# The short convolution of a Mamba block moves from VectorE to TensorE, as four shifted products with scaled weights

## Chip, core and metric

The kernel runs on one core of a Trainium2 chip. The metric is device time in microseconds (us); lower is better. The kernel before took 253.39 us in the median of 3 runs (253.25 to 253.78).

## What is computed

There are 4 sequences of 256 tokens with 256 features (`x`), and a context with 128 features per token (`ctx`). The first half is a Mamba block on the context:

```
x   = einsum('ed,bld->bel', in_proj_w, ctx)           # 128 -> 256 channels
xc  = causal convolution of x along the tokens, 4 taps per channel (depthwise)
u   = silu(xc + conv_b)
dt, B, C = x_proj_w @ u                               # 8 + 16 + 16 rows
delta = softplus(dt_proj_w @ dt + dt_proj_b)
state = state * exp(delta*A) + delta*u*B              # scan over 256 tokens, 16 states per channel
y   = (sum over states of state*C + D*u) * silu(layernorm(x))
x   = x + tanh(g_xattn) * y
```

The second half is a feed-forward part on layernorm(x): 2 shared units and 8 experts of width 176, of which the two best experts of each token count. Its result is added to x with tanh(g_ffn).

The convolution is xc[e, l] = sum over k = 0..3 of conv_w[e, k] * x[e, l - 3 + k]. Since x is itself a product with `in_proj_w`, the same value is the sum over k of (conv_w[e, k] * in_proj_w[e, :]) times ctx of token l - 3 + k.

## The kernel before

The Mamba part is cut into five pieces of tokens: pieces 0 and 1 are the halves (128 tokens) of the first sequence, pieces 2, 3 and 4 the other three sequences (256 tokens each). The 256 channels lie in two halves of 128 partitions. The scan is cut into 64 steps of 128x512 elements, 16 for each sequence; each step is two states for both channel halves and 128 tokens. The feed-forward part works on 8 tiles of 128 tokens with 10 units each ("up" on TensorE, "gate" on ScalarE and VectorE, "mul" on VectorE, "turn" and "down" on TensorE).

Every engine executes its tasks in a fixed order that is written out in the table `ORDER` as `task:number`. An engine never passes a waiting task. Semaphores join the engines.

The tasks that matter here:

- `project:p` (TensorE, L570): 2 products of `win` with `ctx`, one for each channel half, into PSUM. For piece 1 the result begins three tokens early, since the taps look back.
- `project_out:p` (ScalarE, L723): copies from PSUM, scaled by half of the last tap, plus half the bias, into `xh`. It has two instructions.
- `tap0`, `tap1`, `tap2` (VectorE, L907): each adds one shifted tap from PSUM into `xh`, in two instructions. With five pieces there are 30 instructions.
- `tanh_u` (ScalarE, L729) and `silu_u` (VectorE, L917): u = (tanh(xh) + 1) * xh, which is silu since xh holds half the value.
- `xproj`, `dt`, `dt_out`, `soft_exp`, `log_1`, `soft_log`, `log_2`, `delta0`, `delta1`, `delta2`: they give delta and du = delta*u. `xproj` also writes B and C to DRAM, from where they come back broadcast to all partitions (`bb`, `cc`).
- `scan:m`: on ScalarE it stands for the four exponentials of step m + 1 (L704), on GpSimd for the product dbu = du*B of step m + 1 (L1061), and on VectorE for the scan instruction of step m (L953).
- `prod:m`: VectorE's product with C (L963). Its sum is made on TensorE for the first 8 steps (L600) and on GpSimd afterwards (L1104).
- `keep_ends`, `carry`, `fix`: they carry the state from the first half of a sequence into the second.
- `z_stats:i`: mean and variance of `x` of sequence i, on VectorE (L971, L974) and then GpSimd (L1127 to L1133). `z_norm` and `z_gate` use them.
- `variance:t` (VectorE L1010, GpSimd L1149 to L1155), `norm:t` (ScalarE L807) and `to_features:t` (TensorE L635): they bring tile t to the feed-forward part.

At the start SyncE's queue loads `ctx` of the first sequence, small weights, `x` of the first sequence, the other `ctx`, and then the other three `x`. ScalarE's queue loads `win` and then `params`. TensorE runs 6 products of zeros before `project:0`, 11 after `project:1`, and one before `dt:0`.

## Time and profile before

| | value |
|---|---|
| median of 3 runs | 253.39 us |
| profiled execution | 253.55 us, its span 251.7 us |
| TensorE busy | 205.5 us (82%) |
| VectorE busy | 215.0 us (85%) |
| ScalarE busy | 171.2 us (68%) |
| GpSimd busy | 195.3 us (78%) |
| mean granted clock of TensorE | 0.919 |

The profile shows one execution. Busy time is summed over the whole span, though different stretches are limited by different engines, so the shares must be read by stretch. A granted clock of 1.00 is 2.4 GHz, and 0.50 is 1.2 GHz.

### The profile page before, as it was taken

The page shows a single profiled execution, that of the slowest core. Times are in us where ns is not written, and L with a number is a line of the kernel's source. Part 1 is how long each engine was busy: PE and PEld are TensorE (multiplying, and loading weights), DVE is VectorE, ACT ScalarE, POOL GpSimd, SP SyncE. Part 2 cuts the span into 40 slices and gives each one's busy share as a digit, 9 for nine tenths or more (in the row PEclk, how much of TensorE's full clock was granted, in tenths as well). Part 3 has the DMA queues.
Part 4 walks back from the last instruction along what each step waited for, and adds up shares of the span by engine and source line. Part 5 has one row for each costly group of instructions (what it writes and reads, how often), then busy time and mean ns, then how long its engine had stood idle before and what let it go on. Part 6 is the DMA issues. An engine that isn't in the chain of part 4 may idle for free. (4 is left out here: it accounts for less than half of the span.)

```text
span 251.7 us, 3757 instructions
## 1 busy us (share of the span) xinstructions
PE 205.5 (82%) x874; PEld 148.7 (59%) x874; DVE 215.0 (85%) x522; ACT 171.2 (68%) x508; POOL 195.3 (78%) x237
## 2 busy tenths in 40 slices
PE   8534594658669895677996899889999999999995
PEld 4223273434355662345854587568888778788884
DVE  2789999999998989999999999989999999645340
ACT  4579879997758997458757998676775682343220
POOL 0248889999999999999999999999999996510000
PEclk9855579575979999999999999999999999999999
DMA  6496999770490202002209302020300000000000
...
DMA packets 26821, 25.45 MB, mean 101 GB/s; under 512 B 1064, under 2 KB 25904, under 8 KB 26160
## 3 DMA queue, kind: packets, MB, share of 16 engines
...
q10 hardware_dynamic: 288, 0.16, 0.2%
...
HBM read 24.04 MB, written 1.18 MB: 100 GB/s over the span
## 5 line engine op out<-in xcount | busy, mean ns | idle before, releaser
L1061 POOL TENSOR_TENSOR dbu<-du,bb 128x512 f32<-128x512 f32 x64 | 81.3, 1284 | 5.1 <-DVE du L463 3.3
L704 ACT ACTIVATE psA<-delta,aneg 128x127 f32<-128x127 f32 x256 | 78.0, 358 | 5.6 <-DVE psH L953 5.3
L953 DVE TENSOR_TENSOR_SCAN psH<-psA,dbu 128x512 f32<-128x512 f32 x64 | 76.5, 1218 | 1.5 <-POOL dbu L1087 0.4
L667 PE MATMUL psU<-wup,hnT 128*128 128x352 f32 x176 | 63.6, 491 | 12.8 <-DVE hcat L869 8.9
L1104 POOL TENSOR_TENSOR acc<-acc,prod 128x512 f32<-128x512 f32 x42 | 54.5, 1297 | 2.4 <-DVE prod L963 1.8
L545 PE MATMUL psD<-wdn,hT 128*128 128x256 f32 x224 | 52.2, 380 | 0.6 <-issue 0.6
L667 PEld LDWEIGHTS psU<-wup,hnT 128*128 128x128 f32 x176 | 32.8, 200 | 32.8 <-DVE hcat L869 13.6
L833 ACT ACTIVATE tg<-psU 128x176 f32<-128x176 f32 x80 | 24.4, 314 | 36.7 <-PE psU L667 23.9
L545 PEld LDWEIGHTS psD<-wdn,hT 128*128 128x128 f32 x224 | 41.5, 190 | 6.7 <-issue 1.1
L963 DVE TENSOR_TENSOR prod<-psH,cc 128x512 f32<-128x512 f32 x64 | 41.9, 679 | 1.1 <-POOL acc L1104 0.7
L1035 DVE SCALAR_TENSOR_TENSOR ag<-tg,psU 128x176 f32<-128x176 f32 x80 | 25.5, 330 | 15.5 <-ACT tg L833 15.1
L869 DVE SCALAR_TENSOR_TENSOR hcat<-psU,wtok,ag 128x176 f32<-128x176 f32 x64 | 24.2, 395 | 0.9
L840 ACT COPY hT<-psM 128x512 f32<-128x512 f32 (+1 forms) x32 | 16.1, 502 | 11.5 <-PE psM L645 11.0
L678 PE MATMUL psU<-whi,hnhi 128*128 128x352 f32 x56 | 23.3, 415 | 0.2 <-DVE hcat L869 0.2
L645 PE MATMUL psM<-ident,hcat 128*128 128x128 f32 x112 | 18.2, 280 | 2.3 <-ACT hT L840 1.4
L645 PEld LDWEIGHTS psM<-ident,hcat 128*128 128x128 f32 x112 | 13.8, 142 | 7.5 <-issue 2.0
L680 PE MATMUL psU<-whi,hnlo 128*128 128x352 f32 x56 | 18.1, 323 | 0.0
L679 PE MATMUL psU<-wlo,hnhi 128*128 128x352 f32 x56 | 18.0, 322 | 0.0
L600 PE MATMUL psD<-prod,ident 128*128 128x256 f32 x32 | 11.2, 516 | 3.3 <-DVE prod L963 3.3
L663 PE MATMUL psU<-wup,hnT 128*128 128x360 f32 x32 | 12.4, 514 | 0.6 <-ACT hnT L815 0.5
L678 PEld LDWEIGHTS psU<-whi,hnhi 128*128 128x128 f32 x56 | 10.6, 188 | 2.8 <-DVE hcat L869 1.0
L600 PEld LDWEIGHTS psD<-prod,ident 128*128 128x128 f32 x32 | 8.1, 265 | 6.7 <-issue 4.8
(117 smaller groups left out, 282.9 us busy)
## 6 DMA issues: line engine op xcount, KB each, us to landing
...
```

Of the source, the lines that this page charges most:

```text
L545: last = pe.matmul(psD[:, 0:D], hT[0:m, g % HT_RING, c:c + P], wdn[0:m, f, :], start=(f == 0), stop=(f == FB - 1))
L645: last = pe.transpose(psM[0:m, c:c + P], hcat[:, t % 2, f * P:f * P + m], ident[:, :])
L667: last = pe.matmul(dst, hnT[:, b % 2, k, lh * P:(lh + 1) * P], wup[:, j - 1, k, :], start=(k == 0), stop=(k == KT - 1))
L678: pe.matmul(dst, h_hi, w_hi, start=(k == 0), stop=False)
L704: last = act.activation(dst[:, j, h, 1:], delta[:, b % 2, h, l0 + 1:l1], ACT.Exp, scale=aneg[:, h * DS + s0 + j:h * DS + s0 + j + 1])
L833: act.activation(tg[:, i % 2, :], psU[:, i % 2, 0:FF], ACT.Tanh, scale=0.5).then_inc(s_tanh, 1)
L869: last = dve.scalar_tensor_tensor(dst, up, wtok[:, b % 2, lh, j - 2:j - 1], ag[:, unit % 2, :], ALU.mult, ALU.mult)
L953: dve.tensor_tensor_scan(psH[:, i % 2], psA[:, i % DA_RING], dbu[:, i % DBU_RING], 0.0, ALU.mult, ALU.add).then_inc(s_scan, 1)
L963: dve.tensor_tensor(tile(prod[:, i % PROD_RING], i), tile(psH[:, i % 2], i), c.unsqueeze(2).broadcast_to([P, ns, EH, l1 - l0]), ALU.mult). ...
L1035: dve.scalar_tensor_tensor(ag[:, i % 2, :], tg[:, i % 2, :], 1.0, psU[:, i % 2, 0:FF], ALU.add, ALU.mult).then_inc(s_ag, 1)
L1061: pool.tensor_tensor(tile(dbu[:, m % DBU_RING], m), du[:, b % 2, :, l0:l1].unsqueeze(1).broadcast_to(shape), bb[:, b % 2, s0:s0 + ns, l0:l ...
L1104: pool.tensor_tensor(acc[:, total % 2], before, prod[:, i % PROD_RING], ALU.add).then_inc(s_add, 1)
```

## The change

The taps leave VectorE. At the start, `in_proj_w` is multiplied by each of the four taps, two products on VectorE (taps 3 and 1) and two on GpSimd (taps 2 and 0). For this the tap weights are loaded, broadcast to all partitions, into a buffer that the scan uses later. Each projection then issues 8 products instead of 2, four for each channel half. The four add up in PSUM, each with the context shifted by its tap. `project_out` scales by 0.5 and adds the bias, and `tanh_u` waits for it directly. The order table is written anew for all engines except SyncE.

```diff
 "TensorE":
-        project:0 project:1 xproj:0 dt:0 xproj:1 dt:1 project:2 prod:0 prod:1 xproj:2 prod:2 prod:3 prod:4
-        prod:5 dt:2 prod:6 prod:7 y_sum:0 to_tokens:0 to_features:0 project:3 up:0 up:1 up:2 up:3 up:4 xproj:3
+        project:0 project:1 xproj:0 dt:0 xproj:1 dt:1 project:2 prod:0 xproj:2 prod:1 prod:2 prod:3 prod:4 dt:2
+        prod:5 prod:6 prod:7 y_sum:0 to_tokens:0 project:3 to_features:0 up:0 up:1 up:2 up:3 xproj:3 up:4 turn:0
 "ScalarE":
-        load:0 project_out:0 project_out:1 tanh_u:0 xproj_out:0 tanh_u:1 dt_out:0 soft_exp:0 xproj_out:1
-        soft_log:0 dt_out:1 soft_exp:1 soft_log:1 first:0 scan:0 skip:0 project_out:2 scan:1 scan:2 z_norm:0
+        load:0 project_out:0 z_norm:0 project_out:1 tanh_u:0 tanh_u:1 skip:0 xproj_out:0 dt_out:0 soft_exp:0
+        xproj_out:1 soft_log:0 dt_out:1 soft_exp:1 soft_log:1 first:0 scan:0 scan:1 scan:2 z_gate:0
...
+        scan:14 weights_hi:3 norm:0 to_features_out:0 project_out:3 z_norm:1 logits_out:0 gate:0 gate:1 tanh_u:3
+        scan:15 z_gate:1 scan:16 weights_hi:4 scan:17 gate:2 gate:3 decay:1 scan:18 xproj_out:3 gate:4 gate:5
 "VectorE":
-        load:0 tap0:0 tap1:0 tap2:0 silu_u:0 tap0:1 tap1:1 tap2:1 z_stats:0 silu_u:1 z_stats:1 log_1:0 z_stats:2
-        z_stats:3 log_2:0 delta0:0 delta1:0 log_1:1 delta2:0 log_2:1 delta0:1 scan:0 scan:1 delta1:1 keep_ends:0
+        load:0 z_stats:0 z_stats:1 z_stats:2 z_stats:3 silu_u:0 silu_u:1 log_1:0 log_2:0 delta0:0 delta1:0
+        delta2:0 log_1:1 log_2:1 delta0:1 scan:0 scan:1 keep_ends:0 prod:0 prod:1 keep_ends:1 scan:2 delta1:1
+        scan:3 delta2:1 prod:2 prod:3 keep_ends:2 keep_ends:3 silu_u:2 scan:4 scan:5 prod:4 keep_ends:4
+        keep_ends:5 scan:6 prod:5 prod:6 scan:7 keep_ends:6 prod:7 keep_ends:7 scan:8 scan:9 prod:8 z_gate:0
 "GpSimd":
-        z_stats:0 z_stats:1 first:0 scan:0 scan:1 z_stats:2 z_stats:3 scan:2 scan:3 scan:4 scan:5 scan:6 scan:7
+        load:0 z_stats:0 z_stats:1 z_stats:2 z_stats:3 first:0 scan:0 scan:1 scan:2 scan:3 scan:4 scan:5 scan:6
...
-        scan:47 scan:48 prod:45 variance:4 prod:46 fold:5 features_lo:4 prod:47 fold2:5 gate_y:5 scan:49 scan:50
+        scan:47 variance:4 scan:48 prod:45 prod:46 fold:5 features_lo:4 prod:47 fold2:5 gate_y:5 scan:49 prod:49

+        taps = prod[:, 0:2, :].rearrange("p r (k d) -> p (r k) d", d=DI)
+        def scale_tap(engine, k):
+            if k >= 2:
+                engine.wait_ge(d_win, 16)
+                engine.wait_ge(d_taps, 16)
+            engine.tensor_tensor(wk[:, k], win[:, :], taps[:, k], ALU.mult).then_inc(s_wk[k % 2], 1)
 # project, TensorE
-                    dst, lo = entry(i)
                     for h in range(EH):
-                        last = pe.matmul(dst[:, h, :], win[:, h * P:(h + 1) * P], ctx_sb[:, b, lo:l1],
-                                         start=True, stop=True)
+                        for k in reversed(range(DC)):
+                            back = DC - 1 - k
+                            if i == 0 and h == 0:
+                                pe.wait_ge(s_wk[k % 2], 2 - k // 2)
+                            n0 = max(l0, back)
+                            last = pe.matmul(entry(i)[:, h, n0 - l0:], wk[:, k, h * P:(h + 1) * P],
+                                             ctx_sb[:, b, n0 - back:l1 - back], start=(k == DC - 1), stop=(k == 0))
 # ScalarE, ahead of all else
+            act.dma_start(taps[:, :, :], w_taps.unsqueeze(0).broadcast_to([P, DC, DI])).then_inc(d_taps, 16)
             act.dma_start(win[:, :], w_in).then_inc(d_win, 16)
 # project_out
-                        act.activation(xh[:, h, l0:l1], src[:, h, l0 - lo:], ACT.Identity,
-                                       scale=Wh[:, h, DC - 1:DC],
-                                       bias=cwh[:, EH * DC + h:EH * DC + h + 1]).then_inc(s_xh, 1)
+                        act.activation(xh[:, h, l0:l1], entry(i)[:, h, :], ACT.Identity,
+                                       scale=0.5, bias=cwh[:, h:h + 1]).then_inc(s_xh, 1)
 # VectorE: load gets scale_tap(dve, k) for k in (3, 1), GpSimd's new load:0 scale_tap(pool, k) for k in (2, 0)
-                elif task in ("tap0", "tap1", "tap2"):
...
-                        dve.scalar_tensor_tensor(xh[:, h, n0:l1], src[:, h, n0 - back - lo:l1 - back - lo],
-                                                 Wh[:, h, k:k + 1], xh[:, h, n0:l1],
-                                                 ALU.mult, ALU.add).then_inc(s_tap, 1)
```

## Rows read from the trace of the kernel before

**Rows 1.** The page's first part: busy us, share of the span, instructions.
```profile
PE 205.5 (82%) x874; PEld 148.7 (59%) x874; DVE 215.0 (85%) x522; ACT 171.2 (68%) x508; POOL 195.3 (78%) x237
```
**Rows 2.** Windows: stretch and length, busy time by engine, granted clock, DMA share, GB/s.
```profile
52.85:161.00 108.15, 85.70 (x340) 57.89 (x340) 103.34 (x239) 83.93 (x253) 106.20 (x117) 0.95 0.27 88
161.00:222.30 61.30, 59.69 (x297) 48.00 (x298) 56.08 (x148) 37.38 (x119) 52.69 (x68) 1.00 0.09 27
```
**Rows 3.** Timeline of the two hand-overs: start, length, engine, line, what.
```profile
160.99 0.21 POOL L1149 TENSOR_SCALAR ve<-mv 128x1 f32<-128x1 f32 x1
...
220.41 0.60 ACT L807 ACTIVATE hn<-x_sb,nb,rs 128x256 f32<-128x256 f32 x1 [0.27 <-POOL nb L1155]
...
222.30 0.38 PE L635 MATMUL psD<-ident,hn 128*128 128x128 f32 x2
```
**Rows 4.** Timeline of the start, from the projection to GpSimd's products.
```profile
4.45 0.61 PE L570 MATMUL psD<-ctx_sb,win 128*128 128x131 f32 x4
4.65 0.81 ACT L723 ACTIVATE xh<-psM,cwh 128x128 f32<-128x128 f32 x2 [0.36 <-PE psM L570]
...
7.57 0.42 DVE L917 SCALAR_TENSOR_TENSOR u<-psM,xh 128x256 f32<-128x256 f32 x1 [0.45 <-ACT psM L729]
...
9.99 1.28 ACT L731 ACT_TABLE_LOAD   x1
...
10.71 0.74 DVE L971 BATCH_NORM_STATS2 zst<-x_sb 128x6 f32<-128x256 f32 x2
...
15.18 0.39 DVE L932 SCALAR_TENSOR_TENSOR dnc<-dy,psH 128x256 f32<-128x256 f32 x1
...
17.23 3.90 POOL L1061 TENSOR_TENSOR dbu<-du,bb 128x512 f32<-128x512 f32 x3 [3.33 <-DVE du L463]
...
18.71 2.54 DVE L953 TENSOR_TENSOR_SCAN psH<-psA,dbu 128x512 f32<-128x512 f32 x2
...
24.65 4.94 POOL L1061 TENSOR_TENSOR dbu<-du,bb 128x512 f32<-128x512 f32 x4
```
**Rows 5.** Instructions on `xh`: count, ns min/median/max, first and last start.
```profile
L907 DVE SCALAR_TENSOR_TENSOR xh<-psM,cwh,xh x24: 339/470/480, 5.5 to 98.5; 128x253 f32<-128x253 f32 x6, 128x254 f32<-128x254 f32 x6, 128x255 f32<-128x255 f32 x6, 128x125 f32<-128x125 f32 x2
L907 DVE SCALAR_TENSOR_TENSOR xh<-psD,cwh,xh x6: 343/343/343, 7.9 to 9.2; 128x128 f32<-128x128 f32 x6
```
**Rows 6.** GpSimd's waits in 17 to 163 us: total, times, longest.
```profile
POOL dbu L1061 <- DVE psH L953: 1.8, 4, 1.0
```
**Rows 7.** A window (0.50 is the granted clock) and two projections of 256 columns.
```profile
17.20:24.65 7.45, 3.50 (x8) 2.36 (x9) 7.19 (x14) 7.43 (x24) 6.76 (x11) 0.50 0.69 194
...
17.81 2.07 PE L570 MATMUL psM<-ctx_sb,win 128*128 128x256 f32 x4 [3.37 <-DVE dnc L932]
...
89.00 1.03 PE L570 MATMUL psM<-ctx_sb,win 128*128 128x256 f32 x4
```
**Rows 8.** Issue of `x`; us to landing of lines 500 and 477; window 6:7.
```profile
3.42 1.46 SPq L477 DMA_DIRECT2D x_sb<-in_x  x3
...
DMA to landing us min/median/max: 3.5/4.9/10.0
DMA to landing us min/median/max: 4.1/4.3/4.4
6.00:7.00 1.00, 1.00 (x6) 0.47 (x5) 1.00 (x5) 0.16 (x1) 0.00 (x0) 1.00 1.03 343
```
**Rows 9.** Two-input products from SBUF: alone, beside GpSimd, and GpSimd's own.
```profile
15.60 0.42 DVE L452 TENSOR_TENSOR dnc<-drel,dnc 128x256 f32<-128x256 f32 x1
...
17.79 0.99 DVE L452 TENSOR_TENSOR dnc<-drel,dnc 128x256 f32<-128x256 f32 x1
...
118.09 0.73 POOL L1137 TENSOR_TENSOR hnlo<-hnT,hnhi 128x256 fp32r<-128x256 f32 x1
```
**Rows 10.** Timeline of VectorE at `scan:8` and `prod:8`.
```profile
38.07 2.33 DVE L953 TENSOR_TENSOR_SCAN psH<-psA,dbu 128x512 f32<-128x512 f32 x2
...
40.63 1.27 DVE L963 TENSOR_TENSOR prod<-psH,cc 128x512 f32<-128x512 f32 x2
```

More of the change, by code:

```diff
@@ L162 @@
-        z_gate:0 scan:3 tanh_u:2 decay:0 scan:4 scan:5 xproj_out:2 weights_hi:0 scan:6 z_norm:1 scan:7 scan:8
-        dt_out:2 weights_hi:1 soft_exp:2 scan:9 scan:10 soft_log:2 norm:0 scan:11 to_features_out:0 scan:12
-        project_out:3 scan:13 logits_out:0 gate:0 gate:1 z_gate:1 weights_hi:2 weights_hi:3 scan:14 skip:1
-        gate:2 weights_hi:4 scan:15 tanh_u:3 decay:1 scan:16 scan:17 gate:3 gate:4 scan:18 xproj_out:3 hidden:0
-        gate:5 scan:19 scan:20 gate:6 gate:7 hidden:1 scan:21 scan:22 dt_out:3 skip:2 gate:8 gate:9 soft_exp:3
@@ L167 @@
-        scan:23 soft_log:3 norm:1 scan:24 hidden:2 hidden:3 scan:25 scan:26 z_norm:2 to_features_out:1
-        project_out:4 z_gate:2 logits_out:1 gate:10 gate:11 scan:27 scan:28 skip:3 decay:2 tanh_u:4 gate:12
-        scan:29 gate:13 gate:14 scan:30 gate:15 gate:16 scan:31 gate:17 scan:32 hidden:4 hidden:5 scan:33
-        gate:18 gate:19 norm:2 to_features_out:2 features_hi:2 scan:34 scan:35 hidden:6 logits_out:2 gate:20
-        gate:21 scan:36 skip:4 hidden:7 scan:37 scan:38 gate:22 gate:23 xproj_out:4 scan:39 scan:40 gate:24
@@ new lines @@
+        logits_out:1 gate:10 project_out:4 tanh_u:4 skip:3 gate:11 gate:12 gate:13 scan:28 scan:29 gate:14
+        gate:15 scan:30 scan:31 gate:16 hidden:4 hidden:5 decay:2 gate:17 scan:32 gate:18 z_norm:2 gate:19
+        scan:33 scan:34 norm:2 to_features_out:2 features_hi:2 z_gate:2 skip:4 scan:35 logits_out:2 gate:20
+        gate:21 scan:36 hidden:6 hidden:7 gate:22 scan:37 scan:38 gate:23 gate:24 scan:39 xproj_out:4 gate:25
+        scan:40 norm:3 hidden:8 to_features_out:3 gate:26 gate:27 hidden:9 scan:41 scan:42 skip:5 features_hi:3
@@ L195 @@
-        keep_ends:21 mul:7 prod:21 gate_y:1 scan:22 scan:23 gate:8 residual:1 gate:9 stats:1 variance:1
-        keep_ends:22 log_1:3 keep_ends:23 prod:22 prod:23 mul:8 mul:9 log_2:3 scan:24 scan:25 z_gate:1 prod:24
-        prod:25 finish:0 scan:26 scan:27 prod:26 prod:27 tap0:4 gate:10 gate:11 route:1 mul:10 mul:11 gate_y:2
-        tap1:4 tap2:4 scan:28 prod:28 gate:12 mul:12 scan:29 gate:13 scan:30 gate:14 mul:13 mul:14 prod:29
-        residual:2 silu_u:4 stats:2 prod:30 variance:2 gate:15 gate:16 mul:15 scan:31 mul:16 scan:32 prod:31
@@ new lines @@
+        prod:15 scan:17 gate:2 prod:16 gate:3 keep_ends:16 keep_ends:17 mul:2 mul:3 prod:17 scan:18 scan:19
+        keep_ends:18 keep_ends:19 gate:4 gate:5 mul:4 mul:5 gate_y:1 prod:18 prod:19 scan:20 gate:6 gate:7 mul:6
+        mul:7 scan:21 keep_ends:20 prod:20 prod:21 scan:22 gate:8 residual:1 log_1:3 gate:9 stats:1 keep_ends:21
+        scan:23 keep_ends:22 keep_ends:23 log_2:3 mul:8 mul:9 variance:1 prod:22 prod:23 scan:24 prod:24
+        z_gate:1 scan:25 finish:0 prod:25 scan:26 scan:27 prod:26 prod:27 gate_y:2 gate:10 route:1 mul:10
@@ new lines @@
+        keep_ends:37 scan:38 mul:23 scan:39 finish:1 keep_ends:38 gate:24 keep_ends:39 mul:24 prod:38 prod:39
+        gate:25 mul:25 scan:40 scan:41 z_gate:2 gate:26 gate:27 mul:26 prod:40 mul:27 scan:42 prod:41 gate:28
+        gate:29 mul:28 mul:29 prod:42 scan:43 scan:44 log_1:4 residual:4 route:3 stats:4 gate:30 gate:31 log_2:4
+        mul:30 mul:31 prod:43 prod:44 scan:45 variance:4 scan:46 gate:32 gate:33 mul:32 mul:33 prod:45 prod:46
+        scan:47 gate:34 gate:35 mul:34 mul:35 scan:48 finish:2 gate:36 keep_ends:48 prod:47 mul:36 gate:37
@@ L237 @@
+        scan:57 fix:56 fix:57 fix:58 prod:53 features_lo:5 carry:7 prod:54 fold:6 prod:55 scan:58 fold2:6
+        gate_y:6 fix:59 scan:59 scan:60 fix:60 fix:61 prod:57 variance:6 prod:58 prod:59 scan:61 scan:62 fix:62
         fix:63 features_lo:6 prod:60 prod:61 prod:62 fold:7 prod:63 fold2:7 gate_y:7 variance:7 features_lo:7
@@ L1066, in _ @@
             for task, i in order_of("GpSimd"):
-                if task == "first":
+                if task == "load":
+                    for k in (2, 0):
+                        scale_tap(pool, k)
+                elif task == "first":
                     times_b(0)
```

156 lines of the change are left out of this document (69 added, 87 removed).

## The prediction

> **What bounds the kernel now.** I read four views in this order. First the busy shares [rows 1]: VectorE 85%, TensorE 82%, GpSimd 78%, so no engine is full over the whole span, and the question is which one is full when. Second, the windows [rows 2]. From 52.85 to 161 us GpSimd is busy 106.20 of 108.15 us and VectorE 103.34, while TensorE has 22.5 us of idle time. From 161 to 222.3 TensorE is busy 59.7 of 61.3, and afterwards it is nearly alone. So the scan phase goes at the pace of GpSimd with VectorE close behind, and the last 90 us at TensorE's pace. Third, the two hand-overs [rows 3]. TensorE takes up the features of token tile 4 when GpSimd's `variance:4` (160.99) has passed. For the last tile, the normalised tokens are ready at 220.41 + 0.60 = 221.0 and TensorE asks at 222.3: 1.3 us of slack. Fourth, the start [rows 4]: loads, projection, convolution on VectorE, two chains for delta, first scan at 18.71. GpSimd waited 3.33 us for `du` there and began at 17.23, later broke off for the last two `z_stats`, and went on with products at 24.65 (three products end at 21.13). The time to be won or lost is therefore in three places: when the scans begin, what GpSimd has to do before `variance:4`, and TensorE's last stretch.
>
> **The sum is made against** the profiled execution: 253.55 us, its span 251.7 and 1.85 around it. The median of the runs is 253.39, so 0.16 is taken off at the end.
>
> **Removed.** 30 tap instructions on VectorE [rows 5]: 24 at a median of 470 ns and 6 at 343 ns, at most 11.3 + 2.1 = 13.4 us, somewhat less since six of the 24 are half as wide (339 ns): 18 x 0.47 + 12 x 0.34 = 12.5 us. It is the engine beside GpSimd in the scan phase, not GpSimd. GpSimd's waits for VectorE's scans between 17 and 163 us are 1.8 us in four waits [rows 6]: this is all that a faster VectorE can give back directly, besides the start. Inside 52.85 to 161 GpSimd is idle 1.95 us, of which I count half, 0.95, as recovered; the rest are gaps between dependent small instructions.
>
> **Added on TensorE.** Each projection goes from 2 products to 8, each product shows as two instructions, so from 4 to 16. For pieces 0 and 1 (128 columns) four take 0.61 us [rows 4], so 16 take 2.4. For pieces 2 to 4 (256 columns) four take 2.07 us at a granted clock of 0.50 and 1.03 us at full clock [rows 7]: 16 take 8.3 or 4.1 at those rates. That is +6.2, +6.2 and +3.1 us at most, all before 100 us. Projection 3 and 4 lie in TensorE's 22.5 us of idle time and cost nothing if what is queued behind them waits for other things. Behind projection 2 is `prod:0`, and VectorE's `prod:3` needs its ring place back: projection 2 starts when `dnc` of piece 1 is done (just before the first scan, 21), ends at 28 to 29, and `prod:3` is due eight us after the first scan, at 30. It is covered by about 1 us; without that cover the early scans would slip by up to 2 us. Projection 3 now stands ahead of `to_features:0`, whose norm also moves eight positions of scans later, so the feed-forward starts some 8 us later, inside TensorE's idle time. Both ends for the three: 0 and +3; I take 0.
>
> **The start.** The tap weights come by a transfer of 512 KB (4 KB to each of 128 partitions) that is issued first on ScalarE's queue, and `win` and `params` move behind it. No such load is in the trace. The nearest rows are the 512 KB `cc` transfers, 3.5 to 10.0 us from issue to landing, median 4.9 [rows 8]. I take the median: 0.72 + 4.9 = 5.6 us, against `ctx` and `win` at about 3.6 before. Then four scaling products, two on VectorE at 0.42 (a 128x256 product from SBUF, [rows 9]) and two on GpSimd at 0.73 [rows 9]: GpSimd ends last, at 7.1. The last product of half 0 and the four of half 1, 10 instructions, end at 8.6, the ScalarE copies (0.81) at 9.4, projection 1 at 11.1.
> Other things are now ahead of `silu_u:0`. On ScalarE `z_norm:0` stands between the two copies: `z_stats:0` on VectorE at about 7 to 8, its GpSimd part 1.7 us (two in 21.13 to 24.65, [rows 4]), `z_norm` two instructions of about 0.6 (128x256 on ScalarE, [rows 3]), so 10.9; second copy to 11.9, tanh 0.4, 12.3. On VectorE all four `z_stats` stand ahead: they need all of `x`, whose last issue is at 4.4 (three issues of 0.47 from 3.42) and lands 4.4 us later [rows 8], 8.8; the added 512 KB at the 343 GB/s of [rows 8] push this to 10.3; three pairs of statistics with their aggregation at 1.0 us (0.74 for the first two instructions, [rows 4]) end at 13.3. So `silu_u:0` starts at 13.3 instead of 7.57: +5.7 us.
> From there to the first scan it was 11.1 us. The table load of 1.28 us (9.99, ahead of the relus) now lies beside `silu_u:0`: -1.4. `log_2:0` ran at 15.18 behind two pairs of statistics, 2.0 us, of which the logarithm itself hid some 0.6: -1.4. `skip:0` now stands ahead of `xproj_out:0`, partly beside the products that it waits for: +0.4. That is 8.7 us, and the first scan starts at 22.0 instead of 18.71: +3.3 us. Bounds: with `x` not delayed the tanh decides, +2.1; with the taps landing at 10.7, +7.2.
> Here a row and a rule must be weighed. VectorE's two-input product from SBUF took 0.42 us at 15.60 and 0.99 us at 17.79, while GpSimd's product ran [rows 9]. The Trainium skill, "SBUF — State Buffer", section on the shared port pair, says that a VectorE instruction with two SBUF inputs and a GpSimd instruction reading SBUF exclude each other for their whole length. The trace agrees. By it the four scaling products run one after the other, 2.3 us instead of 1.46, and the first projection ends 0.8 us later; the sum stays as it is since the statistics end later still.
>
> **Given back.** The last two `z_stats` of GpSimd (21.13 to 24.65, 3.5 us, [rows 4]) now run before the scans. From the first scan to `scan:8` VectorE has 8 scans at 1.17, 8 products at 0.62 [rows 10], two deltas at 0.42 [rows 9], and an estimated 1.8 for 8 small copies and `silu_u:2`: 17.0 us, where it took 19.4 (18.71 to 38.07). So `scan:8` starts at 39.0, +0.9. `z_gate:0` (0.67) now stands between it and `prod:9`, the first product that GpSimd adds: GpSimd is 1.6 us behind from there, and full again.
> In GpSimd's order `scan:48` and `prod:45` have moved behind `variance:4`: 2 x 1.235 (four in 4.94, [rows 4]; the sums are as wide) = 2.5 us. So `variance:4` comes at 161.0 + 1.6 - 0.95 - 2.5 = 159.1, 1.9 earlier, and TensorE's last phase could end 1.9 earlier. For the last tile no such change of order exists: its tokens come 1.6 - 0.95 = 0.65 later, 221.65, and against TensorE's 222.3 this leaves 0.65. TensorE can thus be early by 0.65 us only. 253.55 - 0.65 = 252.9, less 0.16: **252.7 us**.
>
> **Rivals.**
> 1. *The tap weights land late* (slower). The broadcast shares its queue with `win` and all engines with `x`. The projection chain is T + 1.46 + 1.5 + 2.4 + 0.81 + 0.39 = T + 6.6 to the tanh, so it decides once T passes 6.7 us, and then costs its excess one for one. At the longest 512 KB row, T = 10.7, it is +4.0: 256.7. For it: the transfers are at 1.03 of the engines' time in 6 to 7 us. Against it: the median of 16 such rows is half of that.
> 2. *VectorE was a bound beside GpSimd* (faster). If `x` is not delayed, the start costs only +2.1, 1.2 us less; and if the 12.5 us freed also take away the other 1 us of GpSimd's idle time in 52.85 to 161, the last tile is 2.2 us earlier than in the forecast: 252.7 - 2.2 = 250.5, with TensorE's idle time before 161 as room for it.
> 3. *The late feed-forward stalls the scans* (slower). ScalarE's exponentials of step 16 stand behind `gate:0` and `gate:1`, and these behind projection 3 at half clock. `dnc` of piece 2 comes near 48, 16 instructions at half clock take 6 to 8.3 us, the features, two units and a table load of 1.28 follow, and step 16 comes near 61.5, just when GpSimd's queue wants it. It decides if projection 3 ends after 55; two to three us late would give 255.2. For it: the granted clock fell whenever TensorE had been idle (0.50 at 17.81); against it: TensorE is busy with the sums of products shortly ahead.
>
> **How the numbers follow.** Forecast 0.42, rival 1 0.20, rival 2 0.22, rival 3 0.16. About 0.2% (0.5 us) is what measurement can tell. The forecast's own spread of about 1 us lies half beyond -0.5 and half within; so faster 0.20 + 0.22 = 0.42, same 0.20 + 0.02 = 0.22, slower 0.36. The range reaches from below rival 2 to rival 1: 249.5 to 256.8; the forecast's own is 251.6 to 253.8.
>
> **What would show it.** Taps landing near 5.6 and `silu_u:0` near 13.3; first scan near 22; `scan:8` near 39; GpSimd 1 to 2 us behind at 53 us with under 2 us of idle time up to `variance:4`; `variance:4` near 159; no wait of TensorE at `to_features:7` over 0.7 us; VectorE busy about 203 us. The prediction is wrong if the first scan starts before 20 or after 24, if VectorE shows waits for gates at steps 14 to 17, or if TensorE's idle time after 161 changes by over 1 us.

## The result: 259.4 us, slower, and the profile after

The changed kernel takes 259.36 us in the median of 4 runs (259.08 to 264.56), beside 253.4 us for the kernel before on the same chip. The ratio is 1.023, with a 95% interval of 1.0209 to 1.0251. It is 6.7 us above the forecast of 252.7 and 2.6 us above the end of its range. The profiled execution took 259.2 us, its span is 257.4, so that 1.8 us lie around it. Ratios here leave out disturbed runs; for two experiments (`e3`, `e12`), whose runs and profiles include such ones, the ratio is the figure to use.

The page's first part, which answers to [rows 1]:
```profile
PE 212.7 (83%) x934; PEld 156.8 (61%) x934; DVE 208.4 (81%) x494; ACT 170.2 (66%) x508; POOL 197.4 (77%) x239
```
VectorE lost 6.6 us of busy time, TensorE gained 7.2 and GpSimd 2.1. VectorE was forecast at about 203 us and came to 208.4. Part of this is seen: the taps had kept it busy for 10.8 us and not for the 12.5 of their single lengths, the scaling took 1.3 (0.84 in the forecast), and its scans and products took 1.1 longer in sum. These sums say nothing of the 5.7 us that the span grew by.

The start, which answers to [rows 4] (start us, length, engine, line, operation; in brackets what ended the wait before it):
```profile
6.20 1.29 DVE L402 TENSOR_TENSOR wk<-win,prod 128x256 f32<-128x256 f32 x2 [4.95 <-DMA win<-in_w_in]
6.25 1.83 POOL L402 TENSOR_TENSOR wk<-win,prod 128x256 f32<-128x256 f32 x2 [5.82 <-DMA win<-in_w_in]
...
6.77 3.61 PE L578 MATMUL psM<-ctx_sb,wk 128*128 128x128 f32 x16 [2.86 <-DVE wk L402]
...
10.22 1.95 PE L578 MATMUL psD<-ctx_sb,wk 128*128 128x128 f32 x16
...
10.73 0.75 DVE L964 BATCH_NORM_STATS2 zst<-x_sb 128x6 f32<-128x256 f32 x2 [1.53 <-DMA x_sb<-in_x]
...
12.01 2.54 PE L557 MATMUL psH<-zeros 128*128 128x512 bf16 x11
...
12.73 0.39 ACT L736 ACTIVATE psM<-xh 128x256 f32<-128x256 f32 x1
...
13.52 0.39 DVE L910 SCALAR_TENSOR_TENSOR u<-psM,xh 128x256 f32<-128x256 f32 x1
...
14.48 0.63 PE L588 MATMUL psM<-u,wx 128*40 128x128 f32 x4
...
20.95 6.49 POOL L1054 TENSOR_TENSOR dbu<-du,bb 128x512 f32<-128x512 f32 x5 [4.12 <-DVE du L468]
...
22.21 1.51 DVE L457 TENSOR_TENSOR dnc<-drel,dnc 128x256 f32<-128x256 f32 x1
22.23 6.07 PE L578 MATMUL psM<-ctx_sb,wk 128*128 128x256 f32 x16 [3.15 <-DVE dnc L925]
...
23.65 2.33 DVE L946 TENSOR_TENSOR_SCAN psH<-psA,dbu 128x512 f32<-128x512 f32 x2
```
Read downwards: `u` waits for the last statistics of `x` and starts at 13.52 instead of 7.57; `xproj` waits for the 11 products of zeros, which end at 14.55; the last small product before the scan takes 1.51 us beside GpSimd's, where it took 0.99 before [rows 9]; the first scan starts at 23.65 instead of 18.71.

The same view around `scan:8` (SPq is SyncE's DMA queue; `wup` are the feed-forward's first weights):
```profile
27.18 0.36 SPq L497 DMA_DIRECT2D bb<-brows  x1
...
29.20 2.17 SPq L508 DMA_DIRECT2D wup<-in_w_up  x1
...
41.10 0.78 ACT L832 CAST whi<-wup 128x704 fp32r<-128x704 f32 x1 [5.09 <-DMA wup<-in_w_up]
41.78 2.40 ACT L713 ACTIVATE psA<-delta,aneg 128x127 f32<-128x127 f32 x8
41.95 1.67 POOL L1138 TENSOR_TENSOR wlo<-wup,whi 128x704 fp32r<-128x704 f32 x1 [3.67 <-ACT whi L832]
...
43.05 2.40 DVE L946 TENSOR_TENSOR_SCAN psH<-psA,dbu 128x512 f32<-128x512 f32 x2 [3.32 <-ACT psA L713]
```
ScalarE waited 5.09 us for weights that it only converts. Behind this conversion stand the exponentials of `scan:8` (VectorE waits 3.32) and GpSimd's half of the conversion (waits 3.67). The fetch is issued at 29.20 (at 23.30 before, when ScalarE waited 1.54 us for it) because SyncE's queue has it behind the `bb` and `cc` of the second piece, which move with the start.

**The book of one engine.** GpSimd passes `variance:7`, the last one, at 218.9 before and at 225.6 after. That time is its work up to there plus its idle time up to there. So the loss can be booked by stretch. Windows of the kernel before (stretch, length, busy us of PE, PEld, DVE, ACT, POOL, clock, DMA share, GB/s):
```profile
0.00:21.00 21.00, 12.15 (x46) 6.53 (x46) 14.17 (x47) 13.32 (x37) 6.71 (x15) 0.76 0.68 189
21.00:45.00 24.00, 14.83 (x44) 9.98 (x44) 23.46 (x44) 21.44 (x59) 21.17 (x31) 0.71 0.93 315
45.00:218.91 173.91, 148.34 (x634) 107.56 (x635) 164.74 (x391) 126.99 (x388) 165.44 (x188) 0.95 0.24 78
218.91:251.70 32.79, 30.17 (x151) 24.62 (x150) 12.65 (x43) 9.45 (x28) 1.93 (x5) 1.00 0.02 8
```
And of the changed kernel:
```profile
0.00:21.00 21.00, 13.32 (x66) 8.81 (x66) 9.02 (x33) 10.31 (x27) 7.55 (x23) 0.98 0.47 146
21.00:45.00 24.00, 15.94 (x58) 11.89 (x58) 19.98 (x32) 17.58 (x53) 16.32 (x16) 0.86 0.93 305
45.00:225.60 180.60, 154.37 (x665) 112.24 (x666) 167.61 (x390) 133.29 (x403) 171.57 (x197) 0.95 0.26 85
225.60:257.40 31.80, 29.10 (x147) 23.87 (x145) 11.75 (x41) 8.99 (x27) 1.95 (x5) 1.00 0.03 9
```
The fifth busy number is GpSimd's. Each idle number of this table is a length less that; work is the sum of the first three:

| kernel | work to `variance:7` | idle 0 to 21 | idle 21 to 45 | idle 45 to `variance:7` | from there to the end | span |
|---|---|---|---|---|---|---|
| before | 193.3 | 14.3 | 2.8 | 8.5 | 32.8 | 251.7 |
| changed | 195.4 | 13.5 | 7.7 | 9.0 | 31.8 | 257.4 |
| difference | +2.1 | -0.8 | +4.9 | +0.6 | -1.0 | +5.7 (by the spans) |

So the loss is made before 45 us: 2.1 more work (1.83 of it the two scaling products) and 4.9 us more idle time in 21 to 45. After 45 us GpSimd is as full as before (9.0 us idle against 8.5), though VectorE has less to do.

The hand-over of the last tile, which answers to the second part of [rows 3]:
```profile
225.62 0.21 POOL L1145 TENSOR_SCALAR ve<-mv 128x1 f32<-128x1 f32 x1 [2.46 <-DVE mv L1003]
...
227.12 0.60 ACT L814 ACTIVATE hn<-x_sb,nb,rs 128x256 f32<-128x256 f32 x1 [0.41 <-POOL nb L1151]
...
227.90 0.38 PE L643 MATMUL psD<-ident,hn 128*128 128x128 f32 x2
```
TensorE takes the tokens 0.18 us after they are ready at 227.72, where it had 1.3 us of slack before: the tail came 5.6 us later with GpSimd's delay.

### The profile page after: what moved, and what is told of

Its sections match the earlier page's. It is cut to its first block, busy times and chain, and to the rows that moved or that the text cites. A ratio compares the mean times of both kernels' runs of the same rounds, so it can differ in the third digit from the quotient of the medians.

```text
span 257.4 us, 3843 instructions
## 1 busy us (share of the span) xinstructions
PE 212.7 (83%) x934; PEld 156.8 (61%) x934; DVE 208.4 (81%) x494; ACT 170.2 (66%) x508; POOL 197.4 (77%) x239
## 4 chain that ended last, share of the span: by engine, by line
PE 37%; POOL 27%; issue 17%; DMA 8%; DVE 3%; SPq 3%; ACT 2%; POOLq 0%; ACTq 0%; DVEq 0%
PE psD L550 12%; PE psU L675 10%; POOL acc L1100 10%; POOL dbu L1054 10%; DMA wup<-in_w_up 4%; PE psM L653 3%; DMA brows<-xdbl 3%; PE psU L686 3%; PE psU L688 3%; PE psU L687 2%; PE psU L671 2%; SPq L505 2%; DMA win<-in_w_in 2%; POOL dnc L457 1%; PE psM L578 1%
## 5 line engine op out<-in xcount | busy, mean ns | idle before, releaser
L675 PE MATMUL psU<-wup,hnT 128*128 128x352 f32 x176 | 62.6, 486 | 8.8 <-DVE hcat L872 5.3
L1100 POOL TENSOR_TENSOR acc<-acc,prod 128x512 f32<-128x512 f32 x42 | 53.4, 1272 | 3.2 <-DVE prod L956 2.5
L675 PEld LDWEIGHTS psU<-wup,hnT 128*128 128x128 f32 x176 | 31.8, 196 | 27.5 <-DVE hcat L872 8.1
L1028 DVE SCALAR_TENSOR_TENSOR ag<-tg,psU 128x176 f32<-128x176 f32 x80 | 25.5, 331 | 14.6 <-ACT tg L840 14.3
L578 PE MATMUL psM<-ctx_sb,wk 128*128 128x256 f32 (+7 forms) x64 | 19.8, 488 | 7.9 <-DVE dnc L925 5.1
L578 PEld LDWEIGHTS psM<-ctx_sb,wk 128*128 128x128 f32 x64 | 16.1, 280 | 12.0 <-DVE dnc L925 5.7
L671 PE MATMUL psU<-wup,hnT 128*128 128x360 f32 x32 | 11.3, 476 | 2.7 <-DVE hcat L876 1.7
## 6 DMA issues: line engine op xcount, KB each, us to landing
wup<-in_w_up SPq DMA_DIRECT2D x1, 1760.0 KB, 13.3
```

Source lines behind the costliest of these rows:

```text
L578: last = pe.matmul(entry(i)[:, h, n0 - l0:], wk[:, k, h * P:(h + 1) * P], ctx_sb[:, b, n0 - back:l1 - back], start=(k == DC - 1), stop=(k ...
L675: last = pe.matmul(dst, hnT[:, b % 2, k, lh * P:(lh + 1) * P], wup[:, j - 1, k, :], start=(k == 0), stop=(k == KT - 1))
L1028: dve.scalar_tensor_tensor(ag[:, i % 2, :], tg[:, i % 2, :], 1.0, psU[:, i % 2, 0:FF], ALU.add, ALU.mult).then_inc(s_ag, 1)
L1100: pool.tensor_tensor(acc[:, total % 2], before, prod[:, i % PROD_RING], ALU.add).then_inc(s_add, 1)
```

## The experiments

Each kernel's ratio is to the kernel before, run beside it. The experiments ran on several chips, so two of them are compared by these ratios too, with the 95% range of their difference.

My theory after this reading, S: the start and the late fetch delay GpSimd, which passes the delay on to the end. Its rivals: the longer projections on TensorE, the new order, and a VectorE relief that is worth something.

**e1_old_order.** The changed kernel with the order of before, without taps and with `load:0` on GpSimd.
```diff
-ORDER of the changed kernel
+ORDER of the kernel before, less tap0 to tap2; "GpSimd": load:0 z_stats:0 z_stats:1 first:0 ...
```


> The changed kernel's code with the order table of the kernel before: the tap tasks are taken out, and GpSimd gets its scaling products at its head. It separates the move of the convolution from the new order. Theory S (the loss of 5.9 us is made before the first scan by the tap weights' transfer, the scaling and 16 instructions of the first projection, and the queue of weights behind it): the old order has the same start, so the first scan stays after 23 us and the time stays at 259 or more, up to 263, since GpSimd's last two z_stats come back between the scans (3.5 us). Rival R (the new order is what costs, above all the z_stats ahead of the first silu): the first scan comes before 21 us and the time falls to 254 to 256.

Measured: 266.17 us, ratio 1.051 (1.0486 to 1.0532). Both missed. With this code the new order is 7 us better than the old one. In the old order something costs far more than in the new one; `e8` and `e16` look for it.

**e2_hi_late** and **e5_fetch_early.** Two ways around the wait for `wup`.
```diff
 # e2, ScalarE and GpSimd
-... scan:6 weights_hi:0 scan:7 scan:8 dt_out:2 scan:9 ...
+... scan:6 scan:7 scan:8 dt_out:2 scan:9 weights_hi:0 ...   (GpSimd: weights_lo:0 behind scan:12)
 # e5, SyncE
-xproj:0 dt:0 rows_c:0 rows_c:1 xproj:1 dt:1 rows_c:2 fetch:0
+xproj:0 dt:0 rows_c:0 rows_c:1 xproj:1 fetch:0 dt:1 rows_c:2
```


> The changed kernel with weights_hi:0 moved behind the exponentials of steps 8 to 10 on ScalarE, and weights_lo:0 moved behind the product of step 13 on GpSimd. Nothing else. Theory Q (ScalarE stood 5.1 us waiting for the feed-forward weights that arrive only at 41 us, and the scans with it: 3.3 us on VectorE): the wait is gone from the scans, scan:8 starts near 40 instead of 43, and the time falls by 2 to 3.3 us, to 256 to 257.3. Rival S alone (only the start counts, GpSimd would have been behind anyway): within 0.7 us of the changed kernel, 258.7 to 260.

> The changed kernel with one task of SyncE's queue moved: fetch:0 (the first feed-forward weights) is issued ahead of dt:1, where the queue waits some 5 us for the rows of piece 1 to land. Theory Q: the weights are issued near 23.5 instead of 29.2 and 31.4 and land before 37; ScalarE does not wait for them, scan:8 starts near 40, time 256 to 257.3. Rival: the 1.7 MB then stand in the way of the rows of B and C of piece 1 and of steps 4 to 8, which come 3 to 5 us later, and the time is the same or worse, 259 to 262.

Measured: 258.36 us for `e2` (ratio 1.0208) and 257.9 us for `e5` (1.0186, 1.0152 to 1.0219). By `e5` the late fetch costs about 1.5 us, though GpSimd's wait is 3.67 us long (by the ratios 1.1 us, 0.1 to 2.1); `e5` is 0.6 us above its expectation. Its rival is seen in part: with the fetch first, GpSimd waits 2.0 us for `bb`. `e2` falls between the two expectations, and its gain is within the noise (by the ratios 0.6 us, -0.2 to 1.3). Its profiled start was also later (first scan 25.2). From the first scan to `scan:8` it is 16.8 us in `e5` and 16.2 in `e2`, against 19.4: so both took the wait away.

**e4_no_scaling.** No transfer of tap weights and no scaling; the unscaled `win` stands for all four.
```diff
-            act.dma_start(taps[:, :, :], w_taps...)
-                    for k in (3, 1):
-                        scale_tap(dve, k)
-                             last = pe.matmul(entry(i)[:, h, n0 - l0:], wk[:, k, h * P:(h + 1) * P],
+                             last = pe.matmul(entry(i)[:, h, n0 - l0:], win[:, h * P:(h + 1) * P],
```


> The changed kernel without the transfer of the tap weights and without the four scaling products: all four shifted products take the unscaled projection weights, so the tap weights are left out of the result. TensorE's 8 products for each projection and the order stay. Theory S: ctx and win land near 3.6 again, the first projection ends near 6 instead of 10.4, the last x at 8.8, so the first silu starts near 12 (13.5 with the change) and the first scan near 22 (23.65); the weights come 1.5 to 2 us earlier too; time 255.5 to 257.5. Rival P (TensorE's added products cost): the time stays within 0.7 us of 259.4.

Measured: 257.23 us, ratio 1.0173 (1.0124 to 1.0222), 2.1 us less. As expected. By the ratios it is 1.4 us, with a range of 0.1 to 2.8, since the four runs spread from 255.9 to 258.4. `u` still starts at 12.3, since all statistics stand ahead of it.

**e3_taps_dma_only.** The kernel before plus the transfer alone, first on ScalarE's queue; nothing uses it.
```diff
+            act.dma_start(taps[:, :, :], w_taps.unsqueeze(0).broadcast_to([P, DC, DI])).then_inc(d_taps, 16)
             act.dma_start(win[:, :], w_in).then_inc(d_win, 16)
```


> The kernel before, with the 512 KB transfer of the tap weights issued first on ScalarE's queue and used for nothing (the first product with C waits for it). It prices the transfer alone. Theory S: ctx, win and params land near 6.1 instead of 3.6, everything behind them shifts by 2.5 us, and since GpSimd is full later the time goes up by 2 to 2.5 us, to 255.2 to 255.8. Rival (a start lost on VectorE's convolution chain is made good by idle time before the scans): under 0.7 us.

Measured: ratio 1.0114 (1.0046 to 1.0181), that is about 3 us more than before (1.2 to 4.6). The middle is above both expectations. The transfer alone, without any of its use, costs this kernel about half of what the whole change costs.

**e13_no_scaling_fetch_early.** `e4` and `e5` together.
```diff
 # e4's edit, and SyncE:
-xproj:1 dt:1 rows_c:2 fetch:0
+xproj:1 fetch:0 dt:1 rows_c:2
```


> The changed kernel without the transfer of tap weights and without the scaling (the unscaled win stands for all four taps), and with SyncE's fetch:0 ahead of dt:1. Theory S (late start and late first fetch are separate losses that GpSimd passes on): the gains add, 2.1 + 1.5, 255.8 (255.2 to 256.4), and what is left over before, 2.6 us, is the order. Rival M (the two hide each other, since the wait for the fetch covers the wait for delta): no better than the better of the two alone, 257 to 257.5.

Measured: 255.02 us (254.02 to 255.62), ratio 1.0082 (1.0061 to 1.0104). The losses add: 4.3 us against 2.1 + 1.5, by the ratios 3.7 (2.9 to 4.5) against 1.4 + 1.1. The median is 0.2 us below the expected range, and no excess over the sum is shown. The start of `e13`'s scans:
```profile
21.27 2.33 DVE L943 TENSOR_TENSOR_SCAN psH<-psA,dbu 128x512 f32<-128x512 f32 x2
...
33.56 0.76 ACT L831 CAST whi<-wup 128x704 fp32r<-128x704 f32 x1
...
37.31 2.33 DVE L943 TENSOR_TENSOR_SCAN psH<-psA,dbu 128x512 f32<-128x512 f32 x2
```
No wait stands beside the conversion, and `scan:8` (37.31) follows 16.0 us after the first scan, where it took 19.4. Its window:
```profile
21.00:45.00 24.00, 16.36 (x60) 11.91 (x58) 23.80 (x37) 22.36 (x62) 19.07 (x21) 0.86 1.04 343
```
GpSimd's idle time in 21 to 45 is 4.9 us instead of 7.7. From GpSimd's `variance:0` to the end of the span it is 202.2 us here (50.0 to 252.2), 202.3 in the changed kernel (55.1 to 257.4), 202.2 in `e2` and `e4` and 203.1 in `e5`. What differs between these five was decided before 55 us, but for 0.9 us in `e5`.

**The start is not the same in all of them.** Up to the first scan the changed kernel, `e2`, `e5`, `e10` and `e14` run the same tasks in the same order. Yet `silu_u:0` starts between 13.5 and 15.1, and the first scan between 23.65 (changed kernel) and 25.64 (`e14`). The rows of `e14`:
```profile
7.39 3.85 PE L578 MATMUL psM<-ctx_sb,wk 128*128 128x128 f32 x16 [3.48 <-DVE wk L402]
11.04 3.13 PE L578 MATMUL psD<-ctx_sb,wk 128*128 128x128 f32 x16
...
15.14 0.42 DVE L912 SCALAR_TENSOR_TENSOR u<-psM,xh 128x256 f32<-128x256 f32 x1 [1.45 <-ACT psM L738]
```
The second projection took 3.13 us there and in `e2`, and 1.95 in the other three; then the tanh decides and not the statistics. The granted clock is 1.00 in all of them from 7 to 15 us, so the rows do not show why. Differences of 1 to 2 us between variants of the changed kernel must be read with this in mind.

**e7_no_late_taps.** The kernel before without the 18 tap instructions of pieces 2 to 4.
```diff
-        ... tap0:2 tap1:2 tap2:2 ... tap0:3 tap1:3 tap2:3 ... tap0:4 tap1:4 tap2:4 ...
```


> The kernel before, without the 18 tap instructions of pieces 2, 3 and 4 (left out of the result; 8.5 us of VectorE), all else in the old order. It measures what the relief of VectorE is worth by itself. Theory G (GpSimd sets the pace of the scans): at most the 1.8 us that GpSimd waited for scans, so 252.0 to 253.4. Rival V (VectorE is a second bound): 249 to 251.

Measured: 253.1 us, ratio 0.9998 (0.9977 to 1.0019). The thing that the change is about, less work on VectorE in the scan phase, is worth nothing even when it is free (0.0 us, within 0.5).

**e8_late_on_pe.** Pieces 0 and 1 with taps on VectorE, pieces 2 to 4 with four shifted products on TensorE, in the order of before; the tap weights are loaded last on ScalarE's queue, and GpSimd does the four scaling products before 10.6 us, where it has nothing else to do.
```diff
+                        for k in reversed(range(DC)):
+                            back = DC - 1 - k
+                            last = pe.matmul(dst[:, h, back:], wk[:, k, h * P:(h + 1) * P],
+                                             ctx_sb[:, b, 0:l1 - back], start=(k == DC - 1), stop=(k == 0))
```


> The kernel before, with the convolution on TensorE for pieces 2, 3 and 4 only; pieces 0 and 1 stay on VectorE, the tap weights are loaded last on ScalarE's queue, and GpSimd, idle until 10.6 us, does the four scaling products. Old order. Theory: the start is that of the kernel before to within 0.5 us, and the time is that of the kernel without the late taps plus 0 to 1 us for projection 2 at half clock ahead of prod:0: 252.0 to 254. If TensorE's 12 more products for each piece cost more than hidden, 255 to 257.

Measured: 259.91 us, ratio 1.0246 (1.0196 to 1.0295). Far off both. The start is that of before (first scan 18.68), so the 6.8 us over `e7` come from the longer projections:
```profile
17.79 5.34 PE L580 MATMUL psM<-ctx_sb,wk 128*128 128x256 f32 x16 [3.37 <-DVE dnc L943]
...
18.68 2.54 DVE L964 TENSOR_TENSOR_SCAN psH<-psA,dbu 128x512 f32<-128x512 f32 x2
...
23.17 0.84 ACT L734 ACTIVATE xh<-psM,cwh 128x256 f32<-128x256 f32 x2 [3.05 <-PE psM L580]
...
25.16 2.39 DVE L964 TENSOR_TENSOR_SCAN psH<-psA,dbu 128x512 f32<-128x512 f32 x2 [2.30 <-ACT psA L715]
...
48.14 5.44 PE L580 MATMUL psM<-ctx_sb,wk 128*128 128x256 f32 x16
...
53.62 0.84 ACT L734 ACTIVATE xh<-psM,cwh 128x256 f32<-128x256 f32 x2 [3.50 <-PE psM L580]
...
57.31 0.34 DVE L1046 SCALAR_TENSOR_TENSOR ag<-tg,psU 128x176 f32<-128x176 f32 x1 [5.06 <-ACT tg L844]
```
In the old order ScalarE's copy of the projection stands ahead of exponentials, and TensorE's feed-forward behind the projection. The first holds `scan:2` for 2.30 us, the second VectorE's gate for 5.06 (1.91 in `e7`). GpSimd's `variance:0`, `1`, `2` and `7` come 2.0, 4.8, 5.9 and 6.5 us later than in `e7`: each of the three projections adds its part, the last the least.

**e16_late_on_pe_placed.** `e8` with the projections and their copies moved to where I thought nobody waits.
```diff
 # TensorE: project:3 behind up:1, project:4 behind up:11
 # ScalarE: project_out:2 behind scan:2, project_out:3 behind gate:1, project_out:4 behind gate:11
```


> Pieces 2 to 4 on TensorE in the order of before (259.9), with project:3 moved behind up:1 and project:4 behind up:11 on TensorE, and project_out:2 behind scan:2, project_out:3 behind gate:1, project_out:4 behind gate:11 on ScalarE. Theory Q (the 6.8 us were waits of exponentials and gates behind the longer projections in in-order queues): most of it comes back, 254 to 256.5. Rival W (TensorE's longer work costs wherever it stands): 259 to 260.5.

Measured: 258.35 us, ratio 1.0212 (1.0187 to 1.0238). This is between the two expectations. At most 1.5 of the 6.8 us came back, and the intervals of the two ratios overlap, so not even that is sure. The wait moved:
```profile
56.70 0.84 ACT L734 ACTIVATE xh<-psM,cwh 128x256 f32<-128x256 f32 x2 [3.04 <-PE psM L580]
```
ScalarE again waits 3.04 us, now with conversions, the exponentials of the next step and `gate:2` behind it. That these are in-order waits is seen in the rows; that all 6.8 us are was not shown.

**e11_new_order_old_start** and **e12_new_order_late_on_pe.** `e7` and `e8` with the order of before up to `scan:1` and the new order behind it.
```diff
 # GpSimd (e12 has load:0 ahead)
+z_stats:0 z_stats:1 first:0 scan:0 scan:1 z_stats:2 z_stats:3 scan:2 ... (new order)
 # ScalarE
+... soft_log:1 first:0 scan:0 skip:0 scan:1 scan:2 z_norm:0 z_gate:0 project_out:2 ... (new order)
```


> The kernel before without the 18 taps of pieces 2 to 4 (left out), with the order of before up to scan:1 and the order of the changed kernel afterwards; no transfer of tap weights, no scaling, no added product. The start is that of before (first scan at 18.7). Theory S: variance:0 comes 4.9 us earlier than in the changed kernel, 50.2, and 202.2 + 1.85 us later it ends: 254.2 (253.2 to 255), so the new order alone gains nothing over the 253.1 of the old one. Rival N (the new order is itself better once the start is not late): 250 to 252.

> The kernel before with pieces 2 to 4 on TensorE by four shifted products (whole computation), pieces 0 and 1 with taps on VectorE as before, the tap weights loaded last on ScalarE's queue and scaled on GpSimd ahead of z_stats:0; order of before up to scan:1, order of the changed kernel afterwards. Beside the run before it (same order, late taps left out) it has only TensorE's added products. Theory C (the new order covers them): within 1 us of that run, 253.5 to 255.5. Rival P (they cost as in the old order, 6.8 us): 259 to 261.

Measured: `e11` 257.38 us, ratio 1.017 (1.0146 to 1.0195); `e12` ratio 1.0139 (1.0118 to 1.0161), about 256.7 us. `e11` is above both its expectations, `e12` between its two. An early first scan (19.1) did not help: `scan:8` came 21.0 us later. The fourth scan waited 1.8 us, to 26.17, for a product that stands behind GpSimd's last two statistics; and VectorE waited 1.93 us, to 34.93, for TensorE's sums, which the new order has behind `xproj:2` (no such wait in `e7`). `e12` against `e11` held: in the new order TensorE's added products cost nothing.

**e10_late_taps_out** and **e14_late_taps_out_kept_warm.** The changed kernel with one product instead of four per channel half for pieces 2 to 4, and then with products of zeros in their place.
```diff
-                        for k in reversed(range(DC)):
+                        for k in (reversed(range(DC)) if i < LH else (DC - 1,)):
 # e14 also, ahead of to_features:0
+                    for _ in range(10 if i == 0 else 0):
+                        pe.matmul(psU[:, 0, :], zeros[:, 0:P], zeros[:, :], start=True, stop=True)
```


> The changed kernel with one product per channel half for pieces 2 to 4 (their tap weights 0 to 2 are left out), so TensorE's projections 2 to 4 have 4 instructions instead of 16. Theory C (the new order covers the longer projections, unlike the old one, where the same products cost 6.8 us): no change of more than 0.7 us, 258.6 to 259.8. Rival P (the longer projections cost in the new order too, as in the old one): 252.5 to 255. In between, 256 to 258, means that one of the three projections is uncovered.

> The changed kernel with one product per channel half for pieces 2 to 4 (tap weights 0 to 2 left out there), which took 261.2, plus 10 products of zeros (128x512, into PSUM that nobody reads) between project:3 and to_features:0. Theory K (the added products of project:3 had paid for themselves by keeping TensorE's granted clock up when the first tile's feed-forward started; 0.50 in 56 to 62 us without them, 0.85 with them): back to the time of the changed kernel, 258.8 to 260. Rival O (the loss without them has another cause, the order of waits): stays at 260.8 to 261.8.

Measured: `e10` 261.23 us, ratio 1.0317 (1.0298 to 1.0336): less work on TensorE, and 1.9 us slower than the changed kernel. It missed both expectations. In the window 56 to 62 us of the changed kernel, TensorE's clock (the number behind the five) is 0.85:
```profile
56.00:62.00 6.00, 5.14 (x18) 3.41 (x16) 2.84 (x5) 5.39 (x15) 5.83 (x10) 0.85 1.03 342
```
and in `e10`:
```profile
56.00:62.00 6.00, 3.37 (x7) 1.98 (x8) 2.87 (x3) 4.02 (x10) 6.00 (x7) 0.50 1.03 358
```
TensorE had idled 4.76 us ahead of `to_features:0` and went on at 0.50, that is 1.2 GHz, in the first tile's feed-forward. `e14` took 261.8 us (259.4 to 261.95), so its total is not back: it is where the rival had put it. But its profiled start was late for another reason (first scan 25.6 instead of 23.9, see above). From GpSimd's `variance:0` to the end it takes 203.1 us, `e10` 205.1 and the changed kernel 202.3. So most of the 2.8 us of that stretch came back, with the clock at 0.78. I read this as the clock, but the time itself does not prove it, and the first unit's products still took 2.74 us in `e14` as in `e10` (1.45 in the changed kernel).

**e15_before_kept_warm.** The kernel before with 12 such products ahead of `to_features:0`.
```diff
+                    for _ in range(12 if i == 0 else 0):
+                        pe.matmul(psU[:, 0, :], zeros[:, 0:P], zeros[:, :], start=True, stop=True)
```


> The kernel before with 12 products of zeros (128x512, into PSUM that nobody reads) on TensorE ahead of to_features:0, in its 5.3 us of idle time there. Theory K: the granted clock in 44 to 50 us rises from 0.59, project:3 and up:0 to up:1 take some 2 us less, and if the scans wait for gate:0 it is faster, 251.5 to 252.8. Rival G (the gate is not on the path of GpSimd, which is full there): 252.9 to 253.6. If the products outlast the idle time: up to 254.

Measured: 253.09 us, ratio 1.0000 (0.9986 to 1.0014). The clock in 44 to 50 us rose from 0.59 to 0.78, and nothing waited for it.

**e6_zstats_first** and **e9_start_order.** Two orders of the start: in `e6` the kernel before gets the last statistics ahead of the first `dbu`; in `e9` the changed kernel gets `silu_u` ahead of most statistics.
```diff
 # e6, GpSimd
-z_stats:0 z_stats:1 first:0 scan:0 scan:1 z_stats:2 z_stats:3
+z_stats:0 z_stats:1 z_stats:2 z_stats:3 first:0 scan:0 scan:1
 # e9, VectorE and ScalarE; and 2 instead of 11 products of zeros
-load:0 z_stats:0 z_stats:1 z_stats:2 z_stats:3 silu_u:0 silu_u:1
+load:0 z_stats:0 silu_u:0 silu_u:1 z_stats:1 z_stats:2 z_stats:3
-load:0 project_out:0 z_norm:0 project_out:1 tanh_u:0 tanh_u:1 skip:0 xproj_out:0
+load:0 project_out:0 tanh_u:0 project_out:1 tanh_u:1 z_norm:0 skip:0 xproj_out:0
```


> The kernel before, with GpSimd's z_stats:2 and z_stats:3 moved ahead of its first product; nothing else. They stood in 21.1 to 24.65 us. Theory G: GpSimd starts its products at about 18 instead of 17.2 and has 3.5 us less to do after; if all of it came through, the time would fall by 2.7 us to 250.5. Rival E (in the early scans VectorE sets the pace, GpSimd waits for it anyway): within 0.5 us of 253.2.

> The changed kernel with another order at the start: ScalarE runs project_out:0, tanh_u:0, project_out:1, tanh_u:1 ahead of z_norm:0; VectorE runs z_stats:0, silu_u:0, silu_u:1 ahead of z_stats:1 to 3; TensorE runs 2 instead of 11 products of zeros between project:1 and xproj:0. Theory S (all of the loss is made before GpSimd's variance:0, and from there the span lasts another 202.2 us): silu_u:0 falls from 13.5 to about 10.5, the first scan from 23.65 to 21 to 21.7, and the time from 259.4 to 257 (256.3 to 257.8). Rival F (the late fetch of the first feed-forward weights and B, C sets variance:0, not the start): within 0.6 of the changed kernel, 258.8 to 259.8.

Measured: `e6` 254.56 us, ratio 1.0043 (1.0014 to 1.0072); `e9` 260.8 us, ratio 1.031 (1.0287 to 1.0332). Both are slower than what they started from, and both lie outside their two expectations. In `e9` `silu_u:0` is 2.1 us earlier, and the first scan 1.6 us later (25.2):
```profile
13.28 0.63 PE L588 MATMUL psM<-u,wx 128*40 128x128 f32 x4
...
14.02 1.28 ACT L738 ACT_TABLE_LOAD   x1
...
15.32 1.09 ACT L803 ACTIVATE zn<-x_sb,znb,zrs 128x256 f32<-128x256 f32 x2
...
16.31 0.68 ACT L779 ACTIVATE uD<-u,par 128x128 f32<-128x128 f32 x2
...
16.90 0.24 ACT L745 COPY xdbl<-psM 40x128 f32<-40x128 f32 x1
```
The product is ready at 13.91 and copied at 16.90: the table load, the norm and `skip:0` (3.05 us) had been hidden behind the wait for the statistics. Some 0.9 us of its delay are another matter: its second projection took 2.80 us, against 1.95.

No version tried beats the kernel before.

## Why the prediction was wrong

By its own steps:

- **Which engine sets the pace.** Right. GpSimd is full after 45 us in both kernels, and `e7` shows that the 18 late taps beside it cost nothing. This refutes rival 2's premise, that VectorE was a bound beside GpSimd. The recovered 0.95 us of idle time did not come either: GpSimd's idle time from 45 us to `variance:7` is 9.0 against 8.5.
- **The transfer.** The taps landed at 5.6, as forecast; `win` behind them landed at 6.15, half a microsecond later than the forecast had both. What was underrated is its reach. The chain to the end of the tanh was forecast as T + 6.6; with T = 6.15 that is 12.75, and the tanh ended at 13.12. Two errors cancel in part: scaling and first projection took 1.3 us more than their terms, the second projection and its copy 0.9 less. The statistics decided, as forecast, though only by 0.4 us: `silu_u:0` at 13.52, forecast 13.3. (By the same terms a start without the delay of `x` is 1.0 to 1.1 us earlier, not the 1.2 of the lower bound and of rival 2.)
- **The first scan.** Failed by 1.6 us (23.65, forecast 22.0): from `silu_u:0` 10.1 us, forecast 8.7. Three things were missing from the sum. `xproj:0` waits for the 11 products of zeros (u ready at 13.91, product at 14.48), 0.4 us more than between the same two tasks before. The second piece's chain trails the first by more: its `dnc` starts 1.8 us after the first `delta`, where it was 1.3. And the small product ahead of the scan took 1.51 us beside GpSimd's, 0.5 more than the 0.99 that the 11.1 us contained. Together 1.4 us.
- **From first scan to `scan:8`: 17.0 us.** This is the step that failed most: 19.4 us. The sum counted VectorE's work and left out SyncE's queue and ScalarE's conversion. The fetch of `wup` moved from 23.30 to 29.20, and the wait of 5.09 us for it holds exponentials and GpSimd. Where the wait is gone it is 16.8 (`e5`), 16.2 (`e2`) and 16.0 us (`e13`): the count of VectorE was sound, the missing thing was a queue.
- **GpSimd 1.6 us behind.** At 45 us it was behind by 4.9 - 0.8 + 2.1 = 6.1 us, and the rest of the gap is already there: 4.5 us of mis-sizing here, 1.5 of the idle time that did not come back.
- **`variance:4` at 159.1.** It came at 164.1: 161.0 + 6.1 - 2.5 = 164.6 would be the forecast's own sum with the measured delay, so that the term of the earlier place fits and the delay was the error.
- **The tail.** Nearly right: forecast 1.3 us less from the last tokens to the end, measured 1.0 less from `variance:7`.
- **Projections 2 to 4 at 0 us.** Held in this order (`e12` against `e11`, `e10` even slower without them), and would have been 6.8 us off in the old order (`e8`). I costed them by TensorE's idle time; what decides is which copy and which exponentials stand behind them on ScalarE.
- **Rivals 1 and 3.** Rival 1 named the right object, the transfer, with the wrong mechanism: not the projection chain but everything loaded beside it. By its own mechanism it was close: T came to 6.15 against 6.7, and in `e2` and `e14` the tanh did decide. Rival 3, gates stalling the scans, is seen in `e8`, not in the changed kernel, where VectorE waits 0.8 us for gates from 53 to 85 us (1.6 from 50 to 85 before). Its reason, that the clock fell whenever TensorE had been idle, is not settled by the start of the changed kernel: TensorE idled 2.86 us ahead of its first projection, and the granted clock reads 1.00 from 7 us on, yet the 10 instructions behind the scaling's end took 2.3 us (8.08 to 10.38) and the next 16 took 1.95.

The account of the 6.0 us by experiment: transfer and scaling 2.1 (`e4`), late fetch 1.5 (`e5`), both 4.3 (`e13`). By the ratios the three are 1.4, 1.1 and 3.7, and only the third is known to better than 1 us. About 1.8 us are left over the kernel before (2.1 by the ratio). `e13` still has the new order, its later first scan (21.27 against 18.71) and the longer first two projections, and no run parts these. I tried (`e9`, `e11`) and could not, since each order carries its own start; this stays open.

The Trainium skill, "SBUF — State Buffer", section on the shared port pair, says that a VectorE instruction with two SBUF inputs and a GpSimd one that reads SBUF exclude each other for their whole length. The scaling gives a measure: two products on VectorE and two on GpSimd took from 6.20 to 8.08, 1.88 us. Four on GpSimd took 2.78 in `e8`, 0.70 each, so that full exclusion would make 2 x 0.42 + 2 x 0.70 = 2.2. The trace agrees that they slow each other (0.65 and 0.92 instead of 0.42 and 0.70), but is 0.3 us short of full exclusion; the measured 1.88 us is what counts here.
